# A fused S4 and LSTM block on one Trainium2 core: high and low parts of the second pair of units 16 and 18 a group later in ScalarE's and VectorE's order

## What is computed

```python
x = x + _layernorm(_L0_attn_ref(_layernorm(x, axis=-1), ...), axis=-1)
x = x + _layernorm(_L0_ffn_ref(_layernorm(x, axis=-1), ...), axis=-1)

def step(c, xt):
    ft = jax.nn.sigmoid(xt @ wf.T + c @ uf.T + bf)
    it = jax.nn.sigmoid(xt @ wi.T + c @ ui.T + bi)
    gt = jnp.tanh(xt @ wc.T + c @ uc.T + bc)
    c = ft * c + it * gt
    return (c, None)
c_final, _ = lax.scan(step, c0, x)
h = jnp.tanh(jnp.einsum('tbi,oi->tbo', x, wo) + c_final @ uo.T + bo)
```

## Time and profile before

| | |
|---|---|
| time, median of 3 runs | 2625.73 us (2625.23 to 2626.82) |
| the profiled execution | 2625.0 us, span 2623.2 us |
| PE busy | 2527.6 us, 96% |
| DVE, ACT, POOL busy | 69%, 61%, 42% |
| mean granted clock of PE | 0.988 |
| chain that ended last | PE 84%, DVE 3%, ACT 3% |

### The profile page before, as it was taken

One profiled execution on the slowest core, in us unless ns is written; L12 is line 12 of the kernel. 1 busy time (PEld: TensorE's weight loads), 2 busy tenths in 40 slices (PEclk: granted clock), 3 DMA queues, 4 the chain that ended last, 5 costly groups with the idle time before them and its releaser, 6 DMA issues.

```text
span 2623.2 us, 57588 instructions
## 1 busy us (share of the span) xinstructions
PE 2527.6 (96%) x22739; PEld 2208.3 (84%) x22739; DVE 1813.3 (69%) x3363; ACT 1611.0 (61%) x2985; POOL 1111.6 (42%) x1425
## 2 busy tenths in 40 slices
PE   5599999998999999999999999999999999999998
PEld 4378888887888888888888888888888888888887
DVE  7865656557777777667777877776777764467567
ACT  8766767566555555555556755555555554478768
POOL 7878677724321232222333422322223220068667
PEclk9799999998999999999999999999999999999999
DMA  8879788899855654455547766545665432589988
GB/s 350 327 235 334 265 278 287 286 331 281 235 128 138 149 155 117 113 138 146 164 117 171 196 159 160 134 117 120 138 150 154 117 82 49 183 327 370 354 341 337
DMA packets 504432, 539.91 MB, mean 206 GB/s; under 512 B 269792, under 2 KB 409312, under 8 KB 486112
## 3 DMA queue, kind: packets, MB, share of 16 engines
q1 hardware_dynamic: 504160, 536.23, 66.3%
HBM read 292.35 MB, written 179.83 MB: 180 GB/s over the span
## 4 chain that ended last, share of the span: by engine, by line
PE 84%; DVE 3%; ACT 3%; DMA 1%; POOL 1%; issue 1%; SPq 0%; DVEq 0%; ACTq 0%; POOLq 0%
PE bank L2320 30%; PE bank L2330 29%; PE bank L2377 8%; PE bank L2195 4%; PE bank L2145 3%; PE bank L2203 3%; PE bank L2181 3%; PE bank L2157 2%; PE bank L2352 2%; PE bank L2396 1%; PE bank L2165 1%; DVE big L1987 1%; DMA big<-yd 1%; POOL big L1132 1%; ACT big L1491 0%
## 5 line engine op out<-in xcount | busy, mean ns | idle before, releaser
L2320 PE MATMUL bank<-big 128*128 128x256 f16 x7560 | 1017.9, 273 | 5.7 <-ACT big L1539 4.1
L2330 PE MATMUL bank<-big 128*128 128x256 f16 x7056 | 962.5, 273 | 0.0
L2320 PEld LDWEIGHTS bank<-big 128*128 128x128 f16 x7560 | 739.4, 98 | 92.5 <-ACT big L1539 4.9
L2330 PEld LDWEIGHTS bank<-big 128*128 128x128 f16 x7056 | 690.4, 98 | 79.9
L1131 POOL TENSOR_SCALAR big<-big 128x1 f32<-128x1 f32 x253 | 103.0, 407 | 1100.6 <-DVE big L1839 827.5
L2044 DVE TENSOR_TENSOR big<-bank,big 128x512 f32<-128x512 f32 x240 | 164.1, 684 | 195.5 <-PE bank L2330 190.0
L2377 PE MATMUL bank<-big 128*128 128x256 f16 x2520 | 278.1, 273 | 4.4 <-ACT bank L1460 4.0
L1335 ACT ACTIVATE big<-big 128x512 f32<-128x512 f32 x256 | 206.7, 809 | 114.0 <-POOL big L1133 110.2
L2377 PEld LDWEIGHTS bank<-big 128*128 128x128 f16 x2520 | 246.0, 98 | 35.3 <-ACT bank L1460 4.9
L1404 ACT ACTIVATE big<-big 128x512 f32<-128x512 f32 x360 | 271.4, 803 | 6.3 <-DVE big L2044 6.3
L2030 DVE TENSOR_TENSOR big<-bank,big 128x512 f32<-128x512 f32 x240 | 165.2, 688 | 141.2 <-PE bank L2330 119.5
(11 more groups left out here) (236 smaller groups left out, 3877.7 us busy)
## 6 DMA issues: line engine op xcount, KB each, us to landing
xtd<-big SPq DMA_DIRECT2D x58, 1024.0 KB, 6.4
big<-xr SPq DMA_DIRECT2D x16, 2048.0 KB, 9.9
big<-xg SPq DMA_DIRECT2D x64, 512.0 KB, 7.9
big<-kpad SPq DMA_DIRECT2D x32, 1024.0 KB, 12.2
yd<-big SPq DMA_DIRECT2D x16, 2048.0 KB, 16.8
big<-x SPq DMA_DIRECT2D x128, 256.0 KB, 3.4
x1d<-big SPq DMA_DIRECT2D x128, 256.0 KB, 2.9
big<-x1d SPq DMA_DIRECT2D x64, 512.0 KB, 8.4
```

Source lines behind the costliest of these rows:

```text
L2320: ins = e.matmul(o, WX[2 * g + lw][:, q, kt, 128 * a:128 * a + 128], slot[u % 2][:, part, lx, k0 + kt, :], start=(first and kt == 0 and (l ...
L2330: ins = e.matmul(o, WC[2 * g + lw][:, q, kt, 128 * a:128 * a + 128], cc[unit(u)[1] % 2][:, qc, lx, kt, :], start=False, stop=end, skip_gro ...
```

## The change

Two rows for unit 16 and two for unit 18 in the table `SPECIAL` change; nothing else does.

```diff
-    16: {"dve": (..., (89, 1), (89, 2), (91, 3), (91, 3), (92, 0), (93, 2)),
-        "act": (..., (89, 0), (89, 1), (91, 1), (91, 2), (92, 2), (92, 2))},
+    16: {"dve": (..., (89, 1), (89, 2), (92, 2), (92, 2), (93, 2), (93, 2)),
+        "act": (..., (89, 0), (89, 1), (92, 1), (92, 1), (93, 0), (93, 0))},
```

More of the change, by code:

```diff
@@ L289 @@
         "act": ((16, 2), (17, 0), (17, 0), (17, 1), (17, 1), (17, 2), (17, 2), (17, 2), (17, 2), (18, 0), (18, 1), (18, 1), (19, 0), (19, 1), (19, 1), (19, 2))},
-    16: {"dve": ((86, 2), (86, 2), (87, 0), (87, 0), (87, 2), (87, 2), (88, 0), (88, 3), (88, 3), (88, 3), (88, 3), (88, 3), (89, 1), (89, 2), (91, 3), (91, 3), (92, 0), (93, 2)),
-        "act": ((87, 0), (87, 1), (87, 1), (87, 2), (87, 2), (88, 1), (88, 1), (88, 1), (88, 1), (88, 2), (89, 0), (89, 1), (91, 1), (91, 2), (92, 2), (92, 2))},
+    16: {"dve": ((86, 2), (86, 2), (87, 0), (87, 0), (87, 2), (87, 2), (88, 0), (88, 3), (88, 3), (88, 3), (88, 3), (88, 3), (89, 1), (89, 2), (92, 2), (92, 2), (93, 2), (93, 2)),
+        "act": ((87, 0), (87, 1), (87, 1), (87, 2), (87, 2), (88, 1), (88, 1), (88, 1), (88, 1), (88, 2), (89, 0), (89, 1), (92, 1), (92, 1), (93, 0), (93, 0))},
     17: {"dve": ((93, 3), (94, 3), (94, 3), (95, 3), (95, 3), (95, 3), (96, 2), (96, 3), (96, 3), (96, 3), (97, 1), (97, 3), (97, 3), (98, 0), (98, 2), (98, 2), (98, 2), (98, 2)),
         "act": ((95, 1), (95, 2), (96, 0), (96, 0), (96, 1), (96, 2), (96, 2), (96, 2), (97, 0), (97, 1), (97, 1), (97, 2), (98, 1), (98, 1), (98, 1), (98, 2))},
-    18: {"dve": ((99, 2), (99, 2), (100, 1), (100, 1), (100, 3), (100, 3), (100, 3), (101, 2), (101, 2), (101, 2), (101, 2), (101, 3), (101, 3), (102, 2), (103, 3), (103, 3), (104, 0), (105, 2)),
-        "act": ((100, 0), (100, 1), (100, 1), (100, 2), (100, 2), (101, 0), (101, 1), (101, 1), (101, 1), (101, 2), (101, 2), (102, 1), (103, 1), (103, 2), (104, 2), (104, 2))},
+    18: {"dve": ((99, 2), (99, 2), (100, 1), (100, 1), (100, 3), (100, 3), (100, 3), (101, 2), (101, 2), (101, 2), (101, 2), (101, 3), (101, 3), (102, 2), (104, 2), (104, 2), (105, 2), (105, 2)),
+        "act": ((100, 0), (100, 1), (100, 1), (100, 2), (100, 2), (101, 0), (101, 1), (101, 1), (101, 1), (101, 2), (101, 2), (102, 1), (104, 1), (104, 1), (105, 0), (105, 0))},
     19: {"dve": ((105, 3), (106, 3), (106, 3), (107, 3), (107, 3), (107, 3), (108, 2), (108, 3), (108, 3), (108, 3), (109, 1), (109, 3), (109, 3), (110, 0), (110, 2), (110, 2), (110, 2), (110, 2)),
```

## The result

The changed kernel takes 2636.41 us in the median of 5 runs (2633.40 to 2637.18). The kernel before took 2626.47 in the median of 5 runs, and the ratio of the two is 1.0036 with a 95% interval of 1.0026 to 1.0047. So the change made the kernel slower by 0.36%; the medians differ by 9.9 us. The forecast was 2634.3, with a range of 2630.3 to 2637.5, and the measured median lies in it. The profiled execution took 2634.09 us, its span 2632.3.

The account below looks back on a forecast made before the run. The prediction took PE, executing for 96% of the span, to bound the kernel. Terms of +5.17 (including the early gain of -1.10 and -0.60) and +3.4 for the clock gave +8.6 us, 2634.3, range 2630.3 to 2637.5.

Parts of the forecast that it names:

- What bounds: Scan, units 15 and 17: PE executes for 96% of the span, so only a wait of PE counts.
- First term: Units 15 and 17, group 92 and its counterpart: ACT's gate functions L1404 start earlier, shortening PE's waits; -1.10 and -0.60 us.
- Second term: Units 15 and 17: later load of y delays L1838, L1945 and L1539; PE waits 3.44 us each, together +5.17.
- Third term: Behind PE's two new waits: the clock falls to half for 3.3 us, costing about 1.7 each, +3.4 us.
- the row of 3.39 us from the setup: PE's wait before 51.04 us in the profile before; 3.3 us at the lower clock followed, taken as nearest to the new waits.
- What is late next: Transposes of items 4 to 7 leave SP up to 7 us later, ahead of unit 16's first product; costed at nothing.
- The sum: Whole kernel: +5.17 and +3.4 make +8.6 us, 2634.3 on the median of the runs shown.
- That the clock holds: Rival, behind PE's new waits: the clock holds or falls once; +5.2 to +6.9 us, 2630.9 to 2632.6; chance 0.25.
- A longer landing: Rival, load of y: landing takes 8.3 us instead of 6.8, each wait grows by 1.5; +11.6, 2637.3; chance 0.10.
- the faster side: Rival, units 15 and 17: load of y is covered, leaving -1.7 us, 2624.0; chance 0.12, over 0.2% faster 0.01.

## Why the prediction was right

- **What bounds.** Right: PE was the only engine that counted, and it was moved in units 15 and 17, where its two waits had been.
- **First term, -1.10 and -0.60.** From the start of the run, L1404 began 6.89 us in before (1392.86 less 1385.97) and 5.80 after (1392.78 less 1386.98): 1.09 earlier. In unit 17 it was 0.60. The waits left, 0.51 and 1.15 as recorded, are the forecast 0.5 and 1.1. That the gain in unit 15 came out at 1.1 is partly luck of the profile: against the second profile of before it is 0.6 (a wait of 1.09 less 0.51).
- **Second term, +5.17 with the first in it.** L757 went out 13.68 us after the start of the run (1400.66) against 8.06 before, 5.6 later where 5.4 was forecast; L1838 began 20.34 us after it against a forecast of 20.19. Product 6 of group 94 came 22.57 us into the run (1409.55) where it came 20.08 before (1406.05): +2.49 for 2.34. In unit 17 it was +2.92 for 2.83. Together 5.4. In the three other profiles of the change the two add up to 5.7, 5.8 and 6.2.
- **Third term, +3.4.** In the profile of the change 1.3 and 1.35 (7.38 and 7.41 less 6.06), because part of the low stretch, some 0.6 us each time, fell into the wait itself, where it costs nothing. In the three other profiles it was 1.67 in each unit, close to the forecast 1.7. With unit 16 alone it was 2.9 once. The clock fell behind all eight long waits in the four profiles of the change, so the row of 3.39 us from the setup was the right neighbour. The Trainium skill, "TensorE: Matmul & The Clock Gate", Part 1, states that an idle TensorE falls back to half clock. The traces agree with it for these waits of 3.3 to 4.0 us; behind waits of 1.66 to 1.77 us the clock held, and behind one of 1.96 it fell.
- **What is late next.** Costed at nothing, and nothing is what the profile shows: from the first state product of unit 16 (1409.55 + 7.38 - 0.16 = 1416.77) to the start of unit 17's run at 1475.06 it is 58.29 us, as before (1411.96 to 1470.25). Even in the kernel with only the load later, where the load goes out 2.1 us later still and the transposes behind it, it is 58.30.
- **The sum.** For the profiled pair, 2.49 + 2.92 + 1.32 + 1.35 = 8.1 us, and 1.0 which the scan was late before unit 15; the spans differ by 9.1. The forecast of 8.6 was of the right size for it. The three other profiles of the change add up, in the same way, to 9.0, 9.1 and 9.5 us, and against the second profile of before each sum is 0.5 more. The medians differ by 9.9 and 10.8, which is 0.5 to 1.9 us more than the mean of these sums, 8.9 or 9.4. That unprofiled runs have the clock low for twice as long now and then, as the profile of unit 16 alone had, would do it, but it was not seen in them: this rest is open. The mean clock of a run can't settle it, since a profiled execution with 0.985 had 3.4 us at the lower clock in each unit.
- **The rivals.** That the clock holds: refuted behind waits of 3.3 to 4.0 us, true for one of the two shorter waits, 1.66 and 1.96. A longer landing: once and by less than the rival had, with 4.00 us of wait in place of 3.4. The faster side: its condition was the right one. As soon as L1838 no longer stood ahead of L1945, the first term was left alone, and 2624.53 was measured for the forecast 2624.0 of that rival, though the interval doesn't separate it from no change.

## What to carry to other kernels

Before a step is moved in a written order, look up who waits for its count, the DMA queue's waits above all: here the step gated the load of the next unit, and moving it by one group moved the load by 5.6 us. The slack was 1.6 us: before, L1838 ran 8.26 us behind the issue of the load (1402.29 less 1394.03), and a load needed 6.7. Then ask what stands behind the first user of that load on its engine. Here it was enough to move that user by one group to take the loss away; whether this is better than the kernel before isn't shown. Where the bounding engine would be left idle for long enough to drop its clock, price the stretch behind the wait as well.

## What the runs showed that I had not expected

The clock fell behind a wait of 1.96 us, once, and not behind one of 1.66, 1.74 or 1.77, all in the same dense stream of matmuls; the setup's row of 3.39 alone would not have told this. And behind waits of 3.3 to 4.0 us the stretch at 1.2 GHz was 3.4 us in ten places and 6.9 us in one, which changes the price of one wait from 1.3 to 2.9 us. Behind the two waits of 5.6 us it was some 6.8 us, for a loss of 2.6 and 2.3. So two waits of one length can differ by 1.6 us in what they cost, and a price taken from one row is a sample.
